# Turned tiles moved by one store and three reads, the result store behind them, tile 6 turned on TensorE, and another order of the last steps

## The reference, cut to what matters

```
# block 0
h  = layernorm(x) @ w_in + b_in                       # 96 -> 192
l  = depthwise 3x3 conv(h)
m  = layernorm(0.25 * (four decaying scans of l) + l)
x  = x + m @ w_out + b_out
x  = x + gelu(layernorm(x) @ w1 + b1) @ w2 + b2       # 96 -> 384 -> 96
# block 1
xn = LN3(x);  u = xn @ Wu + bu;  g = sigmoid(xn @ Wg + bg)
h  = 0
for 8 steps: h = g * (h @ A) + (1 - g) * u
x  = x + h
x  = x + gelu(LN4(x) @ mlp_w1 + mlp_b1) @ mlp_w2 + mlp_b2
```

## Time and profile before

| | |
|---|---|
| median of 3 runs | 239.33 us (237.86 to 239.82) |
| the profiled execution | 238.78 us, of which the span of the profile is 236.9 |
| TensorE matmul busy | 224.4 us (95%) |
| DVE, POOL, ACT busy | 184.3, 149.0, 136.8 us (78, 63, 58%) |
| DMA | 9.70 MB, 14.9% of 16 engines on SyncE's queue |
| longest chain by line, step 2 on | POOL's xl (L550) and hs (L557) ahead of TensorE's lines |

### The profile page before, as it was taken

How to read it: one execution, slowest core, us unless ns; L and a number is a source line. 1 busy time by engine, 2 the same in 40 slices (tenths; PEclk the granted TensorE clock), 3 DMA queues, 4 the chain that set the end, 5 groups by cost and what they waited for, 6 DMA issues and landing times.

```text
span 236.9 us, 4147 instructions
## 1 busy us (share of the span) xinstructions
PE 224.4 (95%) x1328; PEld 184.7 (78%) x1328; DVE 184.3 (78%) x464; ACT 136.8 (58%) x307; POOL 149.0 (63%) x179
## 2 busy tenths in 40 slices
PE   8999788999999999999999999999899999998894
PEld 6696657798988888878886886888688776887694
DVE  7699999999999998972579877796778676677321
ACT  5667784969687757574724837364454625340421
POOL 6464796879898878597676627558492909272500
PEclk9999999999999999999999999999999999999679
DMA  3951000000000000000000140504233231212101
GB/s 106 242 155 33 1 0 0 4 0 3 0 1 0 4 0 0 3 0 0 3 0 1 23 114 8 125 1 103 66 94 74 68 102 33 66 36 66 33 17 51
DMA packets 12358, 9.70 MB, mean 41 GB/s; under 512 B 1489, under 2 KB 10929, under 8 KB 12337
## 3 DMA queue, kind: packets, MB, share of 16 engines
q1 hardware_dynamic: 12048, 9.36, 14.9%
q10 hardware_dynamic: 288, 0.09, 0.2%
HBM read 5.51 MB, written 3.93 MB: 40 GB/s over the span
## 4 chain that ended last, share of the span: by engine, by line
PE 46%; issue 22%; POOL 17%; DVE 12%; ACT 2%; POOLq 0%; DVEq 0%; ACTq 0%
PE bank L1507 7%; PE pM L1333 7%; POOL xl L550 6%; POOL hs L557 5%; DVE cA L1048 4%; POOL rs L417 3%; PE pM L1669 3%; DVE cB L1048 2%; PE bank L1550 2%; POOL x4b L428 2%; PE bank L1254 2%; PE bank L1382 2%; PE bank L1449 2%; PE bank L1555 2%; PE pA L1420 2%
## 5 line engine op out<-in xcount | busy, mean ns | idle before, releaser
L1048 DVE SCALAR_TENSOR_TENSOR cA<-pA,cols,cA 128x528 f32<-128x528 f32 x54 | 40.6, 753 | 0.2
L417 POOL TENSOR_TENSOR rs<-var,power 128x4 f32<-128x4 f32 x32 | 32.5, 1016 | 13.0 <-DVE var L939 12.5
L550 POOL TENSOR_TENSOR xl<-xt,xh 96x512 fp32r<-96x512 f32 x12 | 15.3, 1279 | 31.8 <-ACT xh L877 31.8
L1669 PEld LDWEIGHTS pM<-w,hid 128*128 128x128 f32 x192 | 31.5, 202 | 4.6
L1333 PEld LDWEIGHTS pM<-w,hid 128*128 128x128 f32 x192 | 28.4, 191 | 5.7 <-issue 1.0
L1669 PE MATMUL pM<-w,hid 128*128 128x96 f32 x192 | 30.4, 279 | 0.0
L1128 DVE SCALAR_TENSOR_TENSOR q<-th,bank 96x256 f32<-96x256 f32 x48 | 19.2, 412 | 12.9 <-PE bank L1382 12.8
L1333 PE MATMUL pM<-w,hid 128*128 128x96 f32 x192 | 28.9, 266 | 0.0
L1382 PE MATMUL pA<-q,a_half 96*96 96x256 f32 x96 | 27.0, 380 | 0.2 <-DVE q L1128 0.2
L1048 DVE SCALAR_TENSOR_TENSOR cB<-bank,cols,cB 128x256 f32<-128x256 f32 x56 | 26.3, 470 | 0.0
L1507 PE MATMUL bank<-local,mix 128*128 128x384 f32 x64 | 24.8, 497 | 0.1
(11 more groups left out here) (246 smaller groups left out, 605.1 us busy)
## 6 DMA issues: line engine op xcount, KB each, us to landing
moved<-blocks SPq DMA_DIRECT2D x48, 48.0 KB, 1.7
xt<-moved SPq DMA_DIRECT2D x12, 192.0 KB, 2.4
x_all<-in_x SPq DMA_DIRECT2D x8, 192.0 KB, 2.8
out<-y SPq DMA_DIRECT2D x7, 192.0 KB, 2.0
w<-in_w SPq DMA_DIRECT2D x1, 480.0 KB, 5.8
w<-in_w SPq DMA_DIRECT2D x1, 336.0 KB, 3.5
mix<-in_mix SPq DMA_DIRECT2D x1, 256.0 KB, 3.8
out<-y SPq DMA_DIRECT2D x2, 96.0 KB, 2.1
```

The costliest lines, as they stand in the source:

```text
L417: pool.tensor_tensor(rs[:, :], var[:, :], power[:, :], ALU.pow).then_inc(step, 1)
L550: return pool.tensor_tensor(in_place(lo), landed(v), in_place(hi).bitcast(F32), ALU.subtract)
L1048: dve.scalar_tensor_tensor(out=acc, in0=src, scalar=col(f"k{'AB'[grp]}{k}"), in1=acc, op0=ALU.mult, op1=ALU.add).then_inc(s["conv_step"], 1)
L1669: last = pe.matmul(dst, hid1[:, j * TILE + k * P:j * TILE + (k + 1) * P], wc1("m2", j * D, (j + 1) * D), start=j == 0 and (k == 0 if whole ...
```

## The change

Five edits.

1. A turned tile is stored by one DMA of 128 partitions x 384 and read back by three, one for each 32 channels, with pieces of 512 bytes. The count that says a read is complete is 48 instead of 16, that of a store 16 instead of 64.
2. The store of y goes behind the reads of its step.
3. LN4 of tile 6 no longer goes through DRAM (`ln4_beside`): ACT scales its chunks in plain order, TensorE transposes them in step 7 into bank 7, ACT copies them to xh4 and to xt4, and POOL subtracts.
4. At the end TensorE does `m1(0)` of tile 6 ahead of the h transposes of tile 7 and the whole `m2` of tile 6 ahead of the transposes of tile 7.
5. Of the last tile's chunks ACT scales three and DVE one; ACT does so behind the third GELU.

```diff
--- before.py
+++ after.py
@@ -99,6 +99,16 @@
     return isinstance(i, int) and i == k
+def ln4_moved(t):
+    return 0 <= t < TILES - 2
+def ln4_beside(t):
+    return t == TILES - 2
 def is_last(t):
@@ -187,7 +197,7 @@
         xt3, xt4 = sb("xt3", TILE), sb("xt4", TILE)
-        moved3, moved4 = (nc.dram_tensor(f"moved{k}", (D, TILE), F32, kind="Internal").ap() for k in (3, 4))
+        moved3, moved4 = (nc.dram_tensor(f"moved{k}", (P, CHUNKS * D), F32, kind="Internal").ap() for k in (3, 4))
         hid1 = sb("hid1", HJ * TILE)
@@ -358,17 +368,16 @@
                 sp.wait_ge(s[done], a + 1)
-                wait(sp, s[loaded], 16 * a)
-                to = moved.rearrange("(b j) (g n) -> g j b n", b=3, g=4)
-                for g in range(4):
-                    sp.dma_start(to[g], blocks[32 * g:32 * (g + 1), :].rearrange("j (b n) -> j b n", b=3))\
-                      .then_inc(s[stored], 16)
+                wait(sp, s[loaded], 48 * a)
+                sp.dma_start(moved, blocks[:, :]).then_inc(s[stored], 16)
             def load_moved(xt, moved, stored, loaded, free, count, a):
-                sp.wait_ge(s[stored], 64 * (a + 1))
+                sp.wait_ge(s[stored], 16 * (a + 1))
                 wait(sp, s[free], count)
-                sp.dma_start(xt[0:D, :], moved).then_inc(s[loaded], 16)
+                for b in range(3):
+                    sp.dma_start(xt[32 * b:32 * (b + 1), :].rearrange("j (g n) -> j g n", g=4),
+                                 moved.rearrange("(g j) (b n) -> b j g n", g=4, b=3)[b]).then_inc(s[loaded], 16)
             def store_y(t):
@@ -378,14 +387,14 @@
                     store_blocks(blocks3, moved3, "blocks3_done", "moved3_stored", "xt3_loaded", n - VIA_DRAM)
-                if tile_known(p):
-                    store_y(p)
-                if tile_known(m) and not is_last(m):
+                if ln4_moved(m):
                     store_blocks(blocks4, moved4, "blocks4_done", "moved4_stored", "xt4_loaded", m)
...
                     load_moved(xt3, moved3, "moved3_stored", "xt3_loaded", "x3_lo", n if n > VIA_DRAM else 0, n - VIA_DRAM)
-                if tile_known(m) and not is_last(m):
+                if ln4_moved(m):
                     load_moved(xt4, moved4, "moved4_stored", "xt4_loaded", "x4_lo", m, m)
+                if tile_known(p):
+                    store_y(p)
             store_y(TILES - 2)
@@ -574,7 +583,7 @@
                 f, c, m, u = i + 1, i, i - 1, i - 2
-                if tile_known(u) and not is_last(u):
+                if ln4_moved(u):
                     pool.wait_ge(s["x4_split"], u + 1)
@@ -593,6 +602,11 @@
                     add_row(x4b[m % 2][:, :], x4[:, :], rows[:, 2 * D:3 * D], s["x4b_ready"])
+                if ln4_beside(m):
+                    pool.wait_ge(s["x4_copied"], 1)
+                    pool.wait_ge(s["x4_split"], m + 1)
+                    pool.wait_ge(s["hid1_psum"], 3 * m)
+                    split_low(xl4, xt4, xh4).then_inc(s["x4_lo"], 1)
                 ln3_std(i + 3)
@@ -694,7 +708,7 @@
                     else:
-                        act.wait_ge(s["xt3_loaded"], 16 * (f - VIA_DRAM + 1))
+                        act.wait_ge(s["xt3_loaded"], 48 * (f - VIA_DRAM + 1))
                         act.activation(in_place(xh3), landed(xt3), ACT.Copy).then_inc(s["x3_split"], 1)
@@ -863,15 +877,18 @@
                     act.wait_ge(s["x4_ready"], x4_count(m))
-                    wait(act, s["blocks4_done"], m)
+                    wait(act, s["blocks4_done"], min(m, TILES - 2))
                     if is_last(m):
-                        scale_rows(xn4, x4, rs4, s["xn4_ready"], range(2))
+                        act.wait_ge(s["tr4_done"], 1)
+                        scale_rows(xn4, x4, rs4, s["xn4_ready"], range(3))
+                    elif ln4_beside(m):
+                        scale_rows(xn4, x4, rs4, s["xn4_ready"])
                     else:
...
             def split4(u):
-                if tile_known(u) and not is_last(u):
-                    act.wait_ge(s["xt4_loaded"], 16 * (u + 1))
+                if ln4_moved(u):
+                    act.wait_ge(s["xt4_loaded"], 48 * (u + 1))
                     wait(act, s["x4_lo"], u)
@@ -904,14 +921,22 @@
                 gelu(1)
-                normalize4(m)
+                if not is_last(m):
+                    normalize4(m)
                 gelu(2)
                 evac_gu(f)
+                if ln4_beside(m):
+                    act.wait_ge(s["tr4_done"], 1)
+                    act.wait_ge(s["x4_lo"], m)
+                    act.wait_ge(s["hid1_psum"], 3 * m)
+                    act.activation(xh4[0:D, :], bank[7][0:D, :], ACT.Copy).then_inc(s["x4_split"], 1)
+                    act.activation(xt4[0:D, :], bank[7][0:D, :], ACT.Copy).then_inc(s["x4_copied"], 1)
                 if is_last(m):
+                    normalize4(m)
                     wait(act, s["x4_lo"], m)
...
                     for h in range(2):
-                        act.wait_ge(s["tr4_done"], 1 + h)
+                        act.wait_ge(s["tr4_done"], 2 + h)
                         act.activation(xh4[0:D, half(h)], last_bank(h)[0:D, half(0)], ACT.Copy)\
@@ -990,13 +1015,13 @@
                     dve.wait_ge(s["xn3_ready"], 4 * n + 4)
-                    wait(dve, s["moved3_stored"], 64 * (n - VIA_DRAM))
+                    wait(dve, s["moved3_stored"], 16 * (n - VIA_DRAM))
                     dve.transpose(blocks3[:, :], xn3[:, :]).then_inc(s["blocks3_done"], 1)
             def turn_blocks4(m):
-                if tile_known(m) and not is_last(m):
+                if ln4_moved(m):
                     dve.wait_ge(s["xn4_ready"], 4 * m + 4)
-                    wait(dve, s["moved4_stored"], 64 * m)
+                    wait(dve, s["moved4_stored"], 16 * m)
                     dve.transpose(blocks4[:, :], xn4[:, :]).then_inc(s["blocks4_done"], 1)
@@ -1009,9 +1034,9 @@
                 dve.wait_ge(s["ln4_step"], m + 1)
-                dve.wait_ge(s["blocks4_done"], m)
+                dve.wait_ge(s["tr4_done"], 1)
                 dve.wait_ge(s["x4_lo"], m)
-                for k in (2, 3):
+                for k in (3,):
                     dve.tensor_scalar(xn4[:, k * D:(k + 1) * D], x4[:, k * D:(k + 1) * D], rs4[:, k:k + 1], None,
@@ -1598,6 +1623,10 @@
                 pe.wait_ge(s["xn4_ready"], 4 * m + 4)
+                if ln4_beside(m):
+                    pe.wait_ge(s["gelu1_done"], 3 * (m - 1) + 1)
+                    transposes(bank[7], xn4, s["tr4_done"])
+                    return
                 pe.wait_ge(s["x4_ready"], x4_count(m))
@@ -1640,6 +1669,8 @@
                             pe.wait_ge(s["x4_split"], g + 1)
+                            if ln4_beside(g):
+                                pe.wait_ge(s["x4_copied"], 1)
                         w = slice(P * j, P * (j + 1))
@@ -1681,6 +1712,14 @@
                 m2(p, 10, 11)
+                if is_last(m):
+                    m1(0)
+                    h_transposes(m)
+                    m1(1)
+                    m1(2)
+                    m2(g, *range(12))
+                    ln4_transposes(m)
+                    return
                 h_transposes(m)
@@ -1699,15 +1738,14 @@
                     gu(f, 1)
+                if ln4_beside(m):
+                    ln4_transposes(m)
                 for h in range(2):
...
                     m2(g, 6 + h)
-                if is_last(m):
-                    ln4_transposes(m)
-                    m2(g, 8, 9, 10, 11)
             run(pe, body0, body1, turn)
```

More of the change, by code:

```diff
@@ L210, in build @@
             "gu_ready", "step_done", "hs_first", "q_ready", "hs_step", "h8_ready", "trh_done", "x4_ready",
-            "bn4_step", "var4_ready", "ln4_step", "xn4_ready", "x4b_ready", "tr4_done", "x4_split", "x4_lo",
+            "bn4_step", "var4_ready", "ln4_step", "xn4_ready", "x4b_ready", "tr4_done", "x4_copied", "x4_split", "x4_lo",
             "hid1_psum", "gelu1_done", "m2_done", "y_ready", "y_stored")}
```

## The result

The changed kernel took 232.35 us (median of 4 runs, 231.48 to 234.15) beside 239.53 us for the one before (4 runs, 237.86 to 239.82): ratio 0.972, interval 0.965 to 0.980. The forecast was 232.4. Executions more than 1.5% above the fastest of their kernel count as slow and are left out of all ratios and medians here, though not of the ranges and counts of runs. The time is right; of the sum behind it one term was mis-sized, and one cause was wrong.

A forecast was written before the change was run, and what follows sets the result against it. TensorE sets the pace, delayed by late turned tiles. Savings of 3.69 (steady steps), 3.05 (last transposes) and 0.15 (behind them) make 6.9 us: 238.78 becomes 231.9 profiled; the median, 0.55 above, is 232.4 us, range 230.6 to 235.8.

The forecast's parts named there:

- an allowance of 5.83 us: Second half: xh4 may start about 5.8 us behind DVE's block transpose; TensorE pays every us beyond it one to one.
- The chain of 4.8 us: Block transpose's end to xh4: store 2.0, wait 0.05, third read's issue 0.86, landing 1.9; 1.0 inside the allowance.
- by y's place: SyncE's queue: y's store between the turned stores makes the next issue 1.76 us instead of 0.43; moving it removes this.
- Steady part -3.69: Steps 2, 4 and 6 lose 0.94, 1.32 and 1.43 us to late turned tiles; all become 12.34 us, saving 3.69.
- Tile 6 on TensorE +0.5: Step 7: four added transposes cost 0.5 us on the path; the copies and subtraction finish before 218.1, when wanted.
- The new wait of 0.7 ahead of `m2`: The end: m2 of tile 6 needs the bank that y of tile 5 reads, so TensorE stands 0.7 us.
- last transposes -3.05: The end: the last transposes start at 224.1 instead of 227.15, saving 3.05 us, with the added transposes' 0.5 included.
- From the last transposes 9.6: From the last transposes to the span's end: 9.6 us instead of 9.75, saving 0.15, since transposes run at full clock.
- Rival 1, the clock: The end: the granted clock still falls to half, costing 2.8 us (235.2) or 4.3 (236.7); chance 0.13.
- Rival 2, reads one after the other: Steps 2 to 7: three reads don't overlap, the chain takes 7.75 us, the kernel is slower at 243.8; chance 0.05.
- Rival 3, part of the steady gain stays away: The 1.33 pause hits turned transfers or a third read is slow; two or three steps lose 0.5 to 1; 234.5, chance 0.12.
- Rival 4, late reads in all steps and half a clock: Reads late by about 1 us in all six steps plus half the clock loss: change within 1%; chance 0.04.

The follow-up runs named there:

- the first profile: The changed kernel with all five edits, in the profiled execution of its first comparison: 234.15 us.
- y behind alone: The kernel before with only the store of y moved behind the reads: 236.6 us beside 236.6, ratio 0.997.
- old warm-up: Five warm-up matmuls of 256 columns; 18 of 64 columns instead took 243.3 us in the kernel before, 238.26 in the changed one.
- old order: The changed kernel without edit 4, h transposes of tile 7 ahead of tile 6's m1: 230.83 us, then 230.24 beside the changed kernel's 231.30.
- y first: The changed kernel, but DVE writes y of tile 5 ahead of tile 7's statistics: 231.36 us, then 231.03 beside the changed kernel's 231.30.

## Why the prediction was right, step by step

- *TensorE bounds; an allowance of 5.83 us, beyond which every us is paid.* Right: the three late tiles of the first profile cost 0.87, 0.14 and 0.29, each equal to its excess to 0.01 us; in the other profiles losses and excess agree to 0.05 us, and the tiles below it cost nothing.
- *The chain of 4.8 us, "three of the four terms have a row of their own".* Right: 4.76 us where nothing disturbs it, 5.0 to 5.3 in the disturbed profile's good steps. The assumed 1.9 for a read was measured as 1.9 to 2.1. Of the four terms the 0.05 for the wait had no row; it is too small to matter.
- *"the issue behind it takes 1.76 instead of 0.43", by y's place.* Wrong, and the one cause that failed. The pause comes from the instruction packets, stays without y, and moves with TensorE's instruction count. The prediction's own rows spoke against y: no y is stored in step 1 (the first is that of tile 0, in step 3), and yet step 2 loses 0.94. I read a neighbour in the queue as a cause; the same pause in the earlier trace rows could have been checked against the DMA queues at that moment. The sentence that followed, "If the pause isn't tied to that place ... 4.8 becomes 6.1 and the step loses 0.3", is what happened in step 5: 6.12 and 0.29.
- *Steady part -3.69.* By profile -2.4 in the first (step 1's read at 3.8 us is outside what I had for it), -3.7 in the one beside the experiments (61.67 us from step 2 to step 7, against 65.38). The term has the right size, but not for the reason given. "What the chain gains beyond the allowance is worth nothing" is wrong too: the pause is still there (one issue of 0.88 to 1.49 us instead of 0.43 in each of steps 3 and 5, in all nine profiles with one store, three reads and the old warm-up), and the us that the chain became shorter is what absorbs it. Had the chain been left at the allowance, taking y away would have gained nothing, as y behind alone shows. That a wrong cause gave a right term is luck.
- *Tile 6 on TensorE +0.5, ready before 218.1; its copies.* Right: the transposes took 0.44 of TensorE's time (211.79 to 212.23), xh4 took 0.59, xt4 0.58 and xl4 1.27, and all ended before they were wanted.
- *The new wait of 0.7 ahead of `m2`; last transposes -3.05.* Right: 0.80 and -3.09, and y was the wait's cause, as the moved y shows. What I didn't ask is whether edit 4 was the best order: it cost 1.1 us, which the sum can't show, since it compares with the end before, in which tile 6 was late. Edit 1 had removed much of that already: with edits 1 and 2 alone it is 17.98 instead of 19.73 (the clock at 0.50 for 3.4 us instead of 6.8), so that edits 3 to 5 bring only 1.3 of the 3.09, where the sum read as if all of it were theirs. "xh4 took as long as they did, so the gap costs nothing more" was the wrong comparison for edit 4: against the old order with tile 6 in time, the gap costs 0.8. What filled the gap were also four `m2` places (8 matmul instructions), not the eight that the sentence before it has.
- *From the last transposes 9.6.* It was 10.6 in the first profile, with a packet beside the last store, and 9.04 in the others, whose last stores land in 1.7 instead of the 2.0 and 2.2 of before. Mis-sized by 0.6. In the profiled execution the packet hid it; whether it did so in the other three runs isn't known.
- *Rival 1, the clock.* It didn't fall: in the windows of after it is 1.00 from 142 to 224, four transposes more and waits of 0.8 and 0.6 us included, and 0.95 behind that. With edits 1 and 2 alone, where tile 6 keeps TensorE waiting 0.89 and 0.61 us (1.31 and 0.63 in the earlier trace rows), the half clock comes back, from 217.8 to 221.2; the 0.71 is the mean of a window that holds both levels:

```profile
218.00:220.00 2.00, 2.00 (x8) 1.67 (x7) 1.16 (x2) 1.82 (x5) 0.92 (x1) 0.50 0.31 98
220.00:222.00 2.00, 2.00 (x15) 2.00 (x15) 0.00 (x0) 0.24 (x1) 0.00 (x0) 0.71 0.00 0
```

  The Trainium skill's rule on transposes ("TensorE: Matmul & The Clock Gate", Part 4) changed nothing here: the granted clock was 1.00 with four more of them in step 7. That isn't a test of the rule, since matmuls stand on both sides of them.
- *Rival 2, reads one after the other.* The six reads of a step are issued within 2.73 us, 0.4 to 0.5 apart, and away from the packets each lands 1.9 to 2.2 behind its issue. They overlap from issue to landing, and the rival's 3 x 1.9 us fell away. The Trainium skill ("DMA: Bandwidth & Descriptors", Rules for kernel authors) has two transfers to disjoint halves of the partitions serialize, since they share the same engines; read as one landing after the other, as the rival did, the measured reads differ from that, and the measurement decides. Whether their pieces take turns on the engines these times don't show.
- *Rival 3, part of the steady gain stays away* by a pause that moves onto turned transfers, 234.5: this is the profiled execution (234.15), though not the median. It and the forecast are the same kernel on two occasions, so the two weren't rivals but the spread of one case.
- *Rival 4, late reads in all steps and half a clock*: neither was seen.

The gain forecast was 6.9 us. It was 7.2 in the first comparison (239.53 to 232.35), and 5.8 and 6.1 in the two beside the experiments (237.16 to 231.34, 237.4 to 231.30). So the hit to 0.05 us is partly luck: the size of the gain depends on how often before loses its clock and on where the packets fall.

## What to carry to other kernels

If a DMA issue or a landing is a us late at a regular distance, look at what else stood in the DMA queues at that moment, instruction packets above all, before its neighbour in the queue is blamed; and give a chain through DRAM at least the length of one such packet (0.9 to 1.5 us here) of slack. A us that makes a chain shorter than its allowance isn't wasted then. When a change has several edits, work out each against the kernel that has the others: edit 4 looked free beside a late tile 6 and cost 1.1 us once tile 6 was in time. In a tail, keep independent matmuls behind the transposes that start the last evacuation, since they cover the wait for it.

## What the runs showed of the hardware

- TensorE's instructions come in packets of 16 KB on the DMA engines that the kernel uses, 10 or 11 in 230 us, 0.88 to 1.47 us each. A transfer beside one landed up to 1.9 us late (3.8 instead of 1.9; 3.4 instead of 2.0), and SyncE's issue took 0.88 to 1.76 us instead of 0.43, ending 0.34 to 0.40 us behind the packet. They are taken as TensorE's because they moved with the number of its matmuls.
- A packet that fell behind the end of the span (at 229.3 with the old order, at 230.2 with y first) went with 2.5 and 2.8 us around the span; in the changed kernel without one it was 1.83. Seen in these profiles, not tested.
- DVE's scaling of one 128x96 chunk takes 1.00 us beside POOL's x4b and ACT's takes 0.3. With edits 1 and 2 alone DVE does two such chunks in 1.19 us, and POOL's instruction beside them ends 0.94 us in. That DVE's first waits for POOL's to end would fit; it wasn't tested. The rows, with old order:

```profile
217.57 1.00 POOL L437 TENSOR_TENSOR x4b<-x,rows 128x384 f32<-128x384 f32 x1
217.63 1.00 DVE L1040 TENSOR_SCALAR xn<-x,rs 128x96 f32<-128x96 f32 x1 [0.64 <-POOL rs L426]
217.76 0.89 ACT L857 ACTIVATE xn<-x,rs 128x96 f32<-128x96 f32 x3
```
